# A one-block language-model tower: chunk 2's embedding moved forward, three matmuls without a reader at a seam, and the order of a head's output against the last maximum of its step

## The chip, the cores and the metric

The kernel runs on one core of one Trainium2 chip. The metric is the time of one execution in microseconds (us) as the device measures it. Engines are named as in the profile: PE is TensorE (PEld its weight loads), DVE is VectorE, ACT is ScalarE, POOL is GpSimd, SP is SyncE.

## The reference

The input is 2 samples (b = 0, 1) of 2048 token ids. Shortened to what matters:

```python
h = W.T[x] + bias + positional                       # (2, 2048, 128)
# block 1: 8 heads of 16, causal, linear (no softmax)
qkv  = layernorm(h) @ w_qkv
dots = where(causal, q @ k.T * scale, 0)
attn = (dots - cumulative mean) * rsqrt(cumulative variance + EPS) * norm_g + norm_b
h    = h + (where(causal, attn, 0) @ v) @ w_out + b_out
# block 2: 2 heads of 64, softmax, then 8 soft-gated experts
hx   = layernorm(layernorm(h)) * ln_g + ln_b
q, k = l2norm(hx @ Wq), l2norm(hx @ Wk);  v = hx @ Wv
y    = softmax(causal(q @ k.T * scale)) @ v @ Wo
gate = softmax(y @ gate_W + gate_b)
h    = h + sum_e gate_e * (gelu(y @ W1_e + b1_e) @ W2_e + b2_e)
```

## The kernel before

Each engine has its instruction list written out by hand, and the engines meet at semaphores (`wait_ge` before an instruction, `then_inc` behind it). An engine works its list strictly in order, so an instruction that waits holds up everything behind it in the same list. Tokens are cut into NT = 16 chunks of 128 per sample, and a chunk is always handled for both samples.

**Stage A, first block.** Chunk c goes through `embed` (DVE: position added, `bn_stats`, `bn_aggr`), `front` (POOL: variance to reciprocal root, by a power), `normed` (DVE: the normalised rows `xn`), `xn_T` (PE transposition), projections, masked products, sums over earlier chunks and an output projection. From chunk 1 on `step_a(c)` does one chunk on every engine and prepares the next ones: DVE embeds c+2 inside step c, PE transposes c+1. Chunk 0 is different: its attention is worked out directly, in `dtm`, before the loop begins, and chunk 2 is embedded between chunk 0 and `step_a(1)`. `state_out` (DVE, L656) masks the running sum of keys times values, `state_add` (POOL, L264) adds it up, and `coefs` (POOL, first instruction L268, a power on 128x16) makes the coefficients that `outputs` (DVE, L720 to L727) multiplies with. PE's list at this place holds the last 16 narrow matmuls of chunk 0 for sample 1, `busy(1, 1)`, which multiplies the identity with constants into a bank nobody reads, `xn_T(2, 0)`, and then `step_a(1)`, whose first products don't need chunk 2.

**Seam A to B.** The last chunk of the first block and the first chunks of the second block are interleaved by hand. On PE the order is: 16 narrow matmuls for sample 1 of chunk 15, `project2(1)` (four matmuls of 128x384, waiting until ACT has copied the sums of chunk 15 out of their banks, L435), `out_T(14)`, `normed_T(2)`, `out_project(14)`.

**Stage C, second attention.** The 8 items are (c, b): 512 queries of one sample. They are worked through in NSTEP = 80 steps; step s takes one block of 128 keys for one item (items have 4, 4, 8, 8, 12, 12, 16, 16 steps). The softmax's maxima are worked out ahead of their item by `pair_scores` (PE, both heads, banks 3 and 4) and `row_max` (DVE, L866); MSLOT[s] lists which of them belong to step s. PE's order within step s is: `scores(s)`, the early pairs, `values(s-2)` for both heads (LAG = 2), the closing pairs, `out_part`s; from step CLOSE = 36 on the closing pairs come behind the `out_part`s. How many pairs close a step is worked out by

```python
closing = min(len(pairs), 1) if s >= CLOSE else len(pairs) // 2
```

A pair waits until DVE has taken the maximum of the pair before it, since both use banks 3 and 4. `head_out(it)` (DVE, a reciprocal L941 and a product L943 into `och`) takes an item's output out of banks 6 and 7. It stands at step OAT[it] = 5, 9, 17, 25, 37, 49, 65, 81, the step in which PE does the item's last `values`. The next item's first `values`, one step later, wait for it (`o_used`). On DVE one step is: `out_part(…, 5)` (L933), all `row_max` of the step, `head_out`, `out_part` 3 or 4 (the gate, L915 to L928), then the low halves of the probabilities that are DVE's (L974, L976).

**Stage D.** 64 rounds of experts follow, PE bound; nothing there is touched. L1024 is the helper `mm`, so that nearly all matmuls carry this line.

Of the kernel before, what the change touches and what calls it, by code (L numbers as in the profile page):

```python
# [23 lines left out]
CH = 512  # L24
# [19 lines left out]
def tower(nc, ids, emb_rows, consts, consts16, rows, cols, w_qkv, w_out, w_sm, w_o, w_gate, w12_rows, b2, out):  # L44
    with ExitStack() as ctx:
# [187 lines left out]
        def _(pool):  # L233
# [3 lines left out]
            def gather(t0, t1):  # L237
                for t in range(t0, t1):
                    g.indirect_dma_start(out=h_all[:, t, :], out_offset=None, in_=emb_rows,  # L239
                                         in_offset=bass.IndirectOffsetOnAxis(ap=idx[:, t:t + 1], axis=0)  # L240
                                         ).then_inc(GATHERED[t // B], 16)
# [7 lines left out]
            def front(c, par):  # L249
                pool.wait_ge(S["stats"], c + 1)  # L250
                g.tensor_tensor(rs[par][:], mv[par][:, :, 1], ln_eps, ALU.add).then_inc(S["veps"], 1)
                pool.wait_ge(S["veps"], c + 1)
                g.tensor_tensor(rs[par][:], rs[par][:], mhalf[:, 0:B], ALU.pow).then_inc(S["rstd"], 1)
# [7 lines left out]
            def state_add(c):  # L261
                for b in range(B):
                    pool.wait_ge(S["sgc_ready"], 2 * c + b + 1)
                    g.tensor_tensor(sg[:, b], sg[:, b], sgc[:, b], ALU.add).then_inc(S["sg_ready"], 1)  # L264
# [50 lines left out]
            out_bias(0)  # L315
            out_bias(1)
            gather(6, 16)
            coefs(0)
            state_add(0)
            front(2, 0)  # L320

            def step_a(c, nxt, more=2, tail=True):
                if c >= 3:
# [289 lines left out]
        def _(dve):  # L613
# [93 lines left out]
            link(v.tensor_reduce(sm[:, 1, 1], sq[:, 1], AX, ALU.add))  # L707
            dve.wait_ge(S["sq_act"], 1)
            v.tensor_scalar(sm[:, 3], sm[:, 1], inv0, DOT_EPS, ALU.mult, ALU.add).then_inc(S["var_ready"], 1)
            for b in range(B):  # L710
                state_out(0, b, first=True)

            def outputs(c, cur, first=False):
                dve.wait_ge(S["coef"], c + 1 if c < NT - 1 else NT + 1)
# [68 lines left out]
                    normed(c + 2, cur)  # L783
                h1_out(c - 1)

            embed(2, 0)
            normed(2, 0)
            step_a(1, 0, first=True)
            for c in range(2, NT - 2, 2):
                for u in range(2):  # L790
# [155 lines left out]
            for s in range(NSTEP + LAG + 8):  # L946
                if s == 0:
                    unit_qk(NT - 1)
                    low_qk(NT - 2)
                for m in range(LAST):  # L950
                    if s == YAT[m] + DVE_Y[2]:
                        out_part(m, 5)
                two = MSLOT.get(s, ())
                for part in two if two and two[0][0] not in ALONE else two[:1]:
                    row_max(*part, (0, 1))
                if s == 1:
                    low_qk(NT - 1)
                for it in range(len(ITEMS)):
                    if s == OAT[it]:
                        head_out(it)  # L960
                for m in range(LAST):
                    if s - YAT[m] in DVE_Y[:2]:
                        out_part(m, DVE_Y.index(s - YAT[m]) + 3)
                for i in (2 * s, 2 * s + 1):
                    if s < NSTEP and not on_pool(i):
                        lo = STEPS[s][2] * P
                        if rounded(i):
                            dve.wait_ge(S["s_used"], i + 1)
                        else:
                            dve.wait_ge(S["p_ready"], copies(i))  # L970
                        if i >= PR:
                            dve.wait_ge(S["pv_done"], i - PR + 1)
                        if rounded(i):
                            v.tensor_copy(phi[:, i % PR, lo:], p32[:, i % QR, lo:]).then_inc(S["phi_dve"], 1)  # L974
                            dve.wait_ge(S["phi_dve"], sum(rounded(j) for j in range(i + 1)))
                        v.tensor_tensor(plo[:, i % PR, lo:], p32[:, i % QR, lo:], phi[:, i % PR, lo:], ALU.subtract  # L976
                                        ).then_inc(S["plo_dve"], 1)
                if two and two[0][0] in ALONE:
                    row_max(*two[1], (0, 1))
# [40 lines left out]
        def _(pe):  # L1020
# [71 lines left out]
            def busy(bank, n):  # L1092
                for i in range(n):
                    mm(ps[:, bank, :], ident, cst[:, 0:CH])
# [10 lines left out]
            for b in range(B):  # L1105
# [13 lines left out]
                    at = D + h * XW + DA  # L1119
                    last = mm(ps[:, 5 + b, at:at + DA], dtm[:, b, h], kv[0][:, b, h, DA:2 * DA], start=False)  # L1120
                last.then_inc(S["x_ps"], 1)
            busy(1, 1)
            xn_T(2, 0, first=True)

            def step_a(c, nxt, more=True, first=False):
# [89 lines left out]
            for b in range(B):  # L1215
                pe.wait_ge(S["dt_sb"], 2 * c + b + 1)
                for h in range(HA):
                    at = D + h * XW
                    last = mm(ps[:, 5 + b, at:at + XW], dtm[:, b, h], kv[cur][:, b, h], start=False)
                last.then_inc(S["x_ps"], 1)  # L1220
                if b == 0:
                    project2(0, [1])
            project2(1)
            out_T(NT - 2)
            normed_T(2)
# [188 lines left out]
            for s in range(NSTEP + LAG + 6):  # L1414
                if s < NSTEP:
                    scores(s)
                if s < 2:
                    unit_T(NT - 2 + s)
                for i in range(WARM_C.get(s, 0)):
                    mm(ps[:, 5, :], minus16, c16[:, 0:CH])  # L1420
                lone = [(*part, h) for part in MSLOT.get(s, ()) if part[0] in ALONE for h in range(HS)]
                pairs = [part for part in MSLOT.get(s, ()) if part[0] not in ALONE]
                assert not (lone and pairs)
                closing = min(len(pairs), 1) if s >= CLOSE else len(pairs) // 2
                for part in lone[:1]:
                    lone_scores(*part)
                for part in pairs[:len(pairs) - closing]:
                    pair_scores(*part)
                if s in RAT:
                    max_row(RAT[s])  # L1430
                if LAG <= s < NSTEP + LAG:
                    values(s - LAG, 0)
                for part in lone[1:2]:
                    lone_scores(*part)
                if LAG <= s < NSTEP + LAG:
                    values(s - LAG, 1)
                for f in {NSTEP: (0, 1), NSTEP + 1: (2,)}.get(s, ()):
                    up(0, f)
                for part in lone[2:]:
                    lone_scores(*part)  # L1440
                if s < CLOSE:
                    for part in pairs[len(pairs) - closing:]:
                        pair_scores(*part)
                for m in range(LAST):
                    if s - YAT[m] in PE_Y:
                        out_part(m, PE_Y.index(s - YAT[m]) + 1)
                if s >= CLOSE:
                    for part in pairs[len(pairs) - closing:]:
                        pair_scores(*part)


# [88 lines left out]
    return {0: 1, 1: 7, 2: 5}.get(c, 0)  # L1540


def on_pool(i):
    s = i // 2
    if s >= NSTEP - 18:
        return i % 2 == 0
    return i % 2 == 0 or len(MSLOT.get(s, ())) != 1 or s < 16 or s % 2 == 0
# [86 lines left out]
```

## Time and profile before

| | before |
|---|---|
| median of 3 runs | 835.01 us (833.29 to 840.62) |
| profiled execution | 834.53 us |
| its span, first to last instruction | 832.7 us |
| PE busy | 778.6 us, 94% of the span |
| DVE busy | 703.0 us, 84% |
| ACT, POOL busy | 486.5 us, 337.3 us |
| chain that ended last | PE 75%, DVE 12%, issue 5%, POOL 4%, ACT 3% |
| mean granted PE clock | 0.990 |

The span is the time between the first and the last instruction; the profiled execution's own time holds 1.8 us more, around it. The granted clock is the share of TensorE's full clock that it is allowed, 1.00 for 2.4 GHz and 0.50 for 1.2 GHz. The chain is followed back from the last instruction, at each step to what released it.

### The profile page before, as it was taken

How to read it: one execution, taken by the hardware profiler on the slowest of the kernel's cores; microseconds unless marked ns; L12 is line 12 of the kernel's file. 1: busy time of each engine (PE TensorE's matmuls, PEld its weight loads, DVE VectorE, ACT ScalarE, POOL GpSimd, SP SyncE). 2: the span in 40 equal slices, each digit the busy share in tenths (PEclk: the TensorE clock that was granted, in tenths of full speed). 3: DMA queues.
4: the chain of work that ended last, by engine and by line, in shares of the span. 5: the costliest groups of instructions: out<-in, count | busy, mean ns of one | idle time of the engine just before them, and what ended most of it. 6: DMA issues, size and time to landing. Idle time of an engine off the chain costs nothing.

```text
span 832.7 us, 21068 instructions
## 1 busy us (share of the span) xinstructions
PE 778.6 (94%) x8230; PEld 552.5 (66%) x8230; DVE 703.0 (84%) x1575; ACT 486.5 (58%) x1023; POOL 337.3 (41%) x374
## 2 busy tenths in 40 slices
PE   1999999999988889998899999999999999999997
PEld 1568778877755455555556556777777777777775
DVE  3649988999688776777667999999999999999997
ACT  2435555555388667786878767455555555555553
POOL 6638999877575557665766631000000000000000
PEclk9989999999999999999999999999999999999999
DMA  4200111010000000000000000000000000000000
GB/s 132 55 10 20 39 39 27 26 27 14 1 1 1 26 2 2 3 2 2 2 2 3 2 14 2 13 2 14 2 14 2 5 11 9 7 6 11 2 15 13
DMA packets 9666, 12.09 MB, mean 15 GB/s; under 512 B 1856, under 2 KB 6592, under 8 KB 9568
## 3 DMA queue, kind: packets, MB, share of 16 engines
q1 hardware_dynamic: 8544, 8.65, 3.5%
q0 software_dynamic: 1024, 2.10, 0.9%
q8 instruction: 65, 1.06, 0.5%
q14 instruction: 33, 0.27, 0.1%
HBM read 8.65 MB, written 2.10 MB: 13 GB/s over the span
## 4 chain that ended last, share of the span: by engine, by line
PE 75%; DVE 12%; issue 5%; POOL 4%; ACT 3%; DMA 1%; DVEq 0%; ACTq 0%
PE ps L1024 74%; DVE mx L866 2%; POOL ss L345 2%; DVE room L974 2%; DVE room L976 1%; DVE qkn L820 1%; ACT room L592 1%; POOL sm L268 1%; DVE mx L861 1%; DVE ss L805 1%; DMA h_all<-emb_rows,idx 1%; DVE y L701 1%; DVE och L943 1%; PE ps L1032 0%; PE ps L1052 0%
## 5 line engine op out<-in xcount | busy, mean ns | idle before, releaser
L605 ACT ACTIVATE cst<-ps,col 128x512 f32<-128x512 f32 x256 | 175.6, 687 | 157.8 <-PE ps L1024 157.0
L1024 PEld LDWEIGHTS ps<-arena,sq 128*128 128x128 f16 x3072 | 191.9, 98 | 62.0 <-DVE sq L1005 4.9
L1024 PE MATMUL ps<-arena,sq 128*128 128x128 f16 x3072 | 213.1, 219 | 0.3 <-DVE sq L1005 0.2
L1024 PE MATMUL ps<-y,arena 128*128 128x512 f16 x768 | 207.4, 379 | 0.4 <-issue 0.4
L1005 DVE TENSOR_TENSOR sq<-cst,sq 128x512 f16<-128x512 f32 x256 | 176.3, 689 | 4.5
L384 POOL TENSOR_TENSOR room<-room 128x512 f16<-128x512 f32 (+3 forms) x122 | 123.2, 1029 | 74.8 <-ACT room L592 73.9
L999 DVE CAST sq<-cst 128x512 f16<-128x512 f32 x256 | 109.8, 429 | 7.5 <-ACT cst L605 0.5
L583 ACT ACTIVATE room<-ps 128x512 f32<-128x512 f32 (+3 forms) x160 | 76.7, 533 | 43.3 <-PE ps L1024 42.9
L866 DVE TENSOR_REDUCE mx<-ps 128x2 f32<-128x1024 f32 (+2 forms) x64 | 70.2, 1096 | 36.7 <-PE ps L1024 36.5
L1024 PEld LDWEIGHTS ps<-y,arena 128*128 128x128 f16 x768 | 64.5, 98 | 32.0 <-issue 1.2
L992 DVE SCALAR_TENSOR_TENSOR h_all<-ps,gs,h_all 128x128 f32<-128x128 f32 x256 | 77.2, 343 | 0.4 <-PE ps L1024 0.4
L1024 PEld LDWEIGHTS ps<-v,room 128*128 128x128 f16 x1632 | 55.8, 98 | 31.6 <-issue 13.8
L1024 PE MATMUL ps<-v,room 128*128 128x65 f16 (+1 forms) x1632 | 66.2, 195 | 7.7 <-DVE och L943 5.1
L592 ACT CAST room<-room 128x512 f16<-128x512 f32 (+3 forms) x142 | 72.5, 561 | 0.0
L1024 PEld LDWEIGHTS ps<-room,y 128*128 128x128 f32 x512 | 60.9, 192 | 2.7 <-ACT y L467 1.7
L1024 PE MATMUL ps<-room,y 128*128 128x34 f32 (+1 forms) x512 | 60.0, 272 | 0.5 <-ACT y L467 0.5
L268 POOL TENSOR_TENSOR sm<-sm,mhalf 128x16 f32<-128x16 f32 x15 | 43.6, 2908 | 27.5 <-DVE sm L747 22.1
L1024 PE MATMUL ps<-kh,qh 64*128 64x512 f16 (+3 forms) x160 | 33.2, 354 | 10.4 <-DVE mx L866 8.6
L752 DVE TENSOR_TENSOR y<-ps,cst 128x1024 f32<-128x1024 f32 x30 | 36.3, 1211 | 7.5 <-PE ps L1024 7.5
L976 DVE TENSOR_TENSOR room<-room 128x512 f16<-128x512 f32 (+3 forms) x38 | 36.4, 957 | 3.8 <-ACT room L592 3.1
L1024 PE MATMUL ps<-y,room 64*128 64x512 f32 x128 | 39.1, 694 | 0.0
L239 POOL DMA_INDIRECT h_all<-emb_rows,idx x32 | 31.6, 988 | 10.3 <-issue 7.9
(166 smaller groups left out, 1189.5 us busy)
## 6 DMA issues: line engine op xcount, KB each, us to landing
sq<-w_rows SPq DMA_DIRECT2D x13, 256.0 KB, 2.8
out<-h_all SPq DMA_DIRECT2D x32, 64.0 KB, 1.6
cst<-consts SPq DMA_DIRECT2D x1, 896.0 KB, 5.3
h_all<-emb_rows,idx POOLq DMA_INDIRECT x32, 2.6
hxT<-w_rows SPq DMA_DIRECT2D x2, 256.0 KB, 2.7
cst<-consts SPq DMA_DIRECT2D x1, 398.0 KB, 3.7
c<-consts SPq DMA_DIRECT2D x1, 256.0 KB, 5.2
x<-w_rows SPq DMA_DIRECT2D x1, 256.0 KB, 3.0
```

What stands on the lines that cost most here:

```text
L268: g.tensor_tensor(sm[:, 4], sm[:, 3], mhalf[:].rearrange("p (b h) -> p b h", b=B), ALU.pow).then_inc(S["r_ready"], 1)
L384: g.tensor_tensor(plo[:, i % PR, lo:], p32[:, i % QR, lo:], phi[:, i % PR, lo:], ALU.subtract).then_inc(S["plo_pool"], 1)
L583: a.activation(p32[:, i % QR, lo:], ps[:, i % 3, lo:], ACT.Exp).then_inc(S["s_used"], 1)
L592: a.copy(phi[:, i % PR, lo:], p32[:, i % QR, lo:]).then_inc(S["p_ready"], 1)
L605: a.activation(hid[:, f], ps[:, HBANK[f], :], ACT.Gelu_apprx_tanh, bias=col[:, K_B1 + k:K_B1 + k + 1], scale=1.0 / WS).then_inc(S["hid_rea ...
L752: v.tensor_tensor(dtm[:, b], ps[:, 3:5, :].rearrange("p z (h j) -> p (z h) j", j=P), upper.unsqueeze(1).to_broadcast([P, HA, P]), ALU.mult ...
L866: v.tensor_reduce(mx[:, it % 2, r, kb], ps[:, 3:5, 0:w], AX, ALU.max).then_inc(S["sm_used"], 1)
L976: v.tensor_tensor(plo[:, i % PR, lo:], p32[:, i % QR, lo:], phi[:, i % PR, lo:], ALU.subtract).then_inc(S["plo_dve"], 1)
L992: v.scalar_tensor_tensor(hr, ps[:, EBANK[n % 2], r * D:(r + 1) * D], gs[:, m, r, n % E:n % E + 1], hr, ALU.mult, ALU.add).then_inc(S["eo_u ...
L999: v.tensor_copy(hhi[:, f], hid[:, f]).then_inc(S["hhi_ready"], 1)
L1005: v.tensor_tensor(hlo[:, f], hid[:, f], hhi[:, f], ALU.subtract).then_inc(S["hlo_even" if f % 2 == 0 else "hlo_odd"], 1)
L1024: return t_.matmul(o, l, r, start=start, stop=stop, skip_group_check=True)
```

## The change

Three places are edited.

1. Between chunk 0 and `step_a(1)`: DVE embeds chunk 2 between the two `state_out`s of chunk 0 and normalises it behind the second. POOL does `front(2, 0)`, then `state_add(0)`, then `coefs(0)`; before it was the reverse. PE's `busy(1, 1)` ahead of `xn_T(2, 0)` is gone.
2. At the seam PE gets three matmuls of 128x512 in 16 bit into bank 3, which nobody reads, ahead of `project2(1)`.
3. In stage C DVE does `head_out` before the maxima of the closing pairs of its step, where it did it behind them. PE's list is the same; the closing count has become a function. Only steps that have both a `head_out` and a closing pair come out in another order: steps 9, 17, 37 and 49 (items 1, 2, 4 and 5).

```diff
@@ POOL
             gather(6, 16)
+            front(2, 0)
+            state_add(0)
             coefs(0)
-            state_add(0)
-            front(2, 0)
@@ DVE, end of chunk 0
-            for b in range(B):
-                state_out(0, b, first=True)
+            state_out(0, 0, first=True)
+            embed(2, 0)
+            state_out(0, 1, first=True)
+            normed(2, 0)
@@ DVE, ahead of step_a(1)
-            embed(2, 0)
-            normed(2, 0)
             step_a(1, 0, first=True)
@@ DVE, stage C, step s
-                for part in two if two and two[0][0] not in ALONE else two[:1]:
+                early = 1 if two and two[0][0] in ALONE else len(two) - closing(s)
+                for part in two[:early]:
                     row_max(*part, (0, 1))
...
                 for it in range(len(ITEMS)):
                     if s == OAT[it]:
                         head_out(it)
+                if two and two[0][0] not in ALONE:
+                    for part in two[early:]:
+                        row_max(*part, (0, 1))
@@ PE, end of chunk 0
-            busy(1, 1)
             xn_T(2, 0, first=True)
@@ PE, seam
                 if b == 0:
                     project2(0, [1])
+            for i in range(3):
+                mm(ps[:, 3, :], minus16, c16[:, 0:CH])
             project2(1)
@@ 
+def closing(s):
+    parts = [part for part in MSLOT.get(s, ()) if part[0] not in ALONE]
+    return min(len(parts), 1) if s >= CLOSE else len(parts) // 2
```

## Rows read from the trace of the kernel before

**Rows 1.** Page, part 2: granted PE clock in 40 equal slices, in tenths.
```profile
PEclk9989999999999999999999999999999999999999
```

**Rows 2.** Stretches: start:end, length, PE busy (instructions), granted clock, DMA share, GB/s.
```profile
44.98:51.70 6.72, 6.72 (x18) 0.50 0.00 0
...
60.16:72.07 11.91, 11.91 (x81) 1.00 0.03 7
```

**Rows 3.** Timeline, end of chunk 0 (start, length, engine, line, [idle before <-releaser]).
```profile
38.03 2.94 POOL L268 TENSOR_TENSOR sm<-sm,mhalf 128x16 f32<-128x16 f32 x1 [4.68 <-DVE sm L709]
...
40.75 0.44 DVE L656 TENSOR_TENSOR room<-ps,cst 128x272 f32<-128x272 f32 x1 [2.47 <-PE ps L1024]
...
41.11 0.43 DVE L631 TENSOR_TENSOR h_all<-h_all,cst 128x256 f32<-128x256 f32 x1
...
42.20 0.15 DVE L641 BATCH_NORM_AGGREGATE mv<-st 128x2 f32<-128x6 f32 x1
...
43.00 1.10 PE L1024 MATMUL ps<-cst 128*128 128x512 f32 x2
...
43.58 0.71 POOL L253 TENSOR_TENSOR rs<-rs,mhalf 128x2 f32<-128x2 f32 x1
44.32 0.60 DVE L648 TENSOR_SCALAR room<-h_all,mv,rs 128x128 f32<-128x128 f32 x2 [1.97 <-POOL rs L253]
...
44.98 0.69 PE L1032 MATMUL ps<-cst,room 128*128 128x128 f32 x2 [0.88 <-DVE room L648]
...
54.18 0.42 DVE L720 TENSOR_TENSOR room<-room,sm 128x256 f32<-128x256 f32 x1
```

**Rows 4.** Timeline, seam between stages A and B.
```profile
224.72 0.99 ACT L435 COPY room<-ps 128x400 f32<-128x400 f32 x2
...
225.86 2.90 PE L1024 MATMUL ps<-wsm,hxT 128*128 128x384 f32 x4 [0.67 <-ACT room L435]
...
230.53 1.49 PE L1024 MATMUL ps<-wsm,hxT 128*128 128x384 f32 x4
...
232.51 1.03 PE L1024 MATMUL ps<-c 128*128 128x512 f16 x4
```

**Rows 5.** Timeline around step 37, item 4's head_out.
```profile
383.02 1.22 DVE L866 TENSOR_REDUCE mx<-ps 128x2 f32<-128x1024 f32 x1 [0.49 <-PE ps L1024]
...
384.39 0.69 DVE L943 TENSOR_TENSOR och<-ps,rl 128x512 f32<-128x512 f32 x1
...
385.14 0.91 PE L1024 MATMUL ps<-v,room 128*128 128x65 f16 x24 [1.62 <-DVE och L943]
...
385.42 0.52 DVE L928 SCALAR_TENSOR_TENSOR gs<-gt,gl 128x32 f32<-128x32 f32 x1
...
386.41 1.23 DVE L866 TENSOR_REDUCE mx<-ps 128x2 f32<-128x1024 f32 x1 [0.47 <-PE ps L1024]
```

**Rows 6.** Timeline around step 49, item 5's head_out.
```profile
414.29 1.23 DVE L866 TENSOR_REDUCE mx<-ps 128x2 f32<-128x1024 f32 x1 [1.65 <-PE ps L1024]
...
416.27 0.67 DVE L976 TENSOR_TENSOR room<-room 128x384 f16<-128x384 f32 x1
...
416.41 1.15 PE L1024 MATMUL ps<-v,room 128*128 128x65 f16 x24 [1.62 <-DVE och L943]
416.87 0.68 DVE L933 TENSOR_TENSOR h_all<-ps,h_all 128x512 f32<-128x512 f32 x1
...
418.15 1.23 DVE L866 TENSOR_REDUCE mx<-ps 128x2 f32<-128x1024 f32 x1 [0.60 <-PE ps L1024]
```

**Rows 7.** Stretches behind both head_outs, columns as in the second group.
```profile
416.41:420.53 4.12, 4.12 (x62) 0.59 0.00 0
385.14:387.69 2.55, 2.33 (x57) 1.00 0.02 6
```

**Rows 8.** Timeline around step 10, behind item 1's head_out.
```profile
309.74 0.23 PE L1024 MATMUL ps<-kh,qh 64*128 64x128 f16 x2 [0.78 <-DVE mx L866]
...
310.58 0.91 PE L1024 MATMUL ps<-v,room 128*128 128x65 f16 x24 [0.50 <-DVE och L943]
```

More of the change, by code:

```diff
@@ L1423, in _ @@
                 assert not (lone and pairs)
-                closing = min(len(pairs), 1) if s >= CLOSE else len(pairs) // 2
+                close = closing(s)
                 for part in lone[:1]:
                     lone_scores(*part)
-                for part in pairs[:len(pairs) - closing]:
+                for part in pairs[:len(pairs) - close]:
                     pair_scores(*part)
@@ L1441, in _ @@
                 if s < CLOSE:
-                    for part in pairs[len(pairs) - closing:]:
+                    for part in pairs[len(pairs) - close:]:
                         pair_scores(*part)
@@ L1447, in _ @@
                 if s >= CLOSE:
-                    for part in pairs[len(pairs) - closing:]:
+                    for part in pairs[len(pairs) - close:]:
                         pair_scores(*part)
```

## The prediction

> **What bounds the kernel now.** I read the page first. PE is busy nearly all the time, and the chain that ended last is PE for three quarters, so a gain must take idle time out of PE, or time at the low clock. The clock row shows one slice of 40 at 8 tenths ([rows 1]), 41 to 62 us, which is where edit 1 sits; single slices hide shorter drops, so I asked for the clock by stretches of 1 us over the whole span. Four places are below full clock: from about 44.9 to 51.7, from 225.7 to 229.2, from 416.9 to 420.3, and the last 3 us. The first three begin within about a microsecond of the end of a PE wait or inside one, and each of these waits is at one of the three edits. Then I read the chain in order of time at these places, and the timeline for who queues behind whom.
>
> **Edit 1, end of chunk 0.** In the chain POOL's power of `coefs(0)` (38.03, 2.94 us) is followed by its three small products, `state_add`, and then `front`'s power (43.58, 0.71 us), on which `normed` on DVE waits (1.97 us idle) and on that `xn_T(2)` on PE, at 44.98 after 0.88 us of idleness ([rows 3]). So the reader of chunk 2 waits for work it does not need. New order: `state_out(0, 0)` on DVE is done by about 38.3, `embed(2)` takes 1.24 us (41.11 to the end of the last aggregate at 42.35), so the statistics exist at 39.5; POOL is idle from its last gather until then, and `front` takes about 1.0, to 40.6. `state_out(0, 1)` still waits for PE until 40.75 and ends at 41.19, so the embedding lies in a 2.47 us wait of DVE and costs nothing there. `normed(2)` (0.60) ends at 41.8. PE comes free at 43.00, where the filler now starts, so PE is next to be late, not DVE: `xn_T(2)` starts at 43.0 instead of 44.98, a gain of **1.98**. Removing the filler costs nothing by itself, it lay in the wait.
>
> What is pushed back is `coefs(0)`: behind `front` and both `state_add`s, the second of which waits for `state_out(0, 1)`; it starts at about 42.0 and ends about 3.9 later, at 45.8 (before 41.9). Its reader is `outputs(0)`, which ran at 54.18 and will come at about 49, since two masked products and two `state_out`s stand ahead of it; 3 us of cover. If that cover were gone, PE would wait at `out_T(0)`, which comes about 10 us after `xn_T(2)`. Behind `coefs(0)` on POOL stands `state_add(1)`, whose input exists at about 46.3: covered by 0.5 us.
>
> The clock: after the gap PE works 6.72 us at 1.2 GHz, all of it busy ([rows 2]). From 44.98 to the second step's first product at 60.16 it is 15.18 us. The same list one step later, with one transposition and one step of products, takes 11.91 us at full clock ([rows 2]). Without the gap I take the full clock: **3.27** less. (Check: 6.72 us at half clock is 3.36 us of work.) The bounds of this term are 0, if the clock falls all the same, and 3.27. I take the upper, since later waits of PE at this loop's rate keep the clock. Each step of stage A is PE bound, so both terms last to the seam. Edit 1: 5.25.
>
> **Edit 2, seam.** `project2(1)` waits 0.67 us for ACT's two copies (224.72, 0.99 us) and then its four matmuls need 225.86 to 228.55, 2.69 us until the next one starts. The same four begin at 230.53 and are followed at 231.86, 1.33 us, at full clock ([rows 4]). The three fillers: four of their kind take 1.03 us with the last one's latency, a pitch of 0.22, so three take 0.65, which fills the wait almost exactly. Cost 0, at worst 0.1 if the copies end early. Gain if they keep the clock: 2.69 - 1.33 = **1.36**. All that follows (ACT's squares, DVE's sums, POOL's roots) hangs on this projection and moves with it. Bounds: if the clock falls anyway, the fillers themselves take 3 x 0.43 = 1.3 at half clock against a wait of 0.67, a loss of 0.6.
>
> The trace and the Trainium skill differ here. The row shows a drop beginning 0.55 us into a wait of 0.67 us ([rows 4]). The Trainium skill, page "TensorE: Matmul & The Clock Gate", section "Why this matters for your kernels", allows PE idle gaps several times as long as these before throughput drops. By it neither gap would be a cause, and fillers would buy nothing; the time that this gives is one of the rivals below.
>
> **Edit 3, head_out first.** Two cases. *Steps 9, 17, 37:* the closing pair waits on PE for the early maximum, so DVE is idle 0.49 before the closing maximum (383.02), and `head_out` could fit there; it takes 0.92 (384.16 to 385.08, the product alone 0.69). Put first, it delays the closing maximum by 0.92 - 0.49 + 0.03 = 0.46, and the next item's `values`, now at 385.14 after 1.62 of waiting, can start when the scores before them end, at 383.5, a gain of 1.6 on PE ([rows 5]). But PE meets DVE again at the next pair: DVE ends the closing maximum at 384.63, does the gate's three instructions (end 385.94 now, 0.94 in all) and starts the next maximum at 385.6 instead of 386.41. Of 1.6 us **0.8** is left. At steps 9 and 17 PE has an early pair ahead of `values`: it waits for the closing maximum (309.74) and would wait to 310.2, with `values` right behind it at about 310.45 instead of 310.58 ([rows 8]). **0.1** each; the gain on one side is eaten by the delay on the other. *Step 49:* one pair, behind everything, and DVE idle 1.65 before it (414.29). `head_out` fits in whole, no maximum is delayed, and `values` go from 416.41 to 414.85, 1.56 ([rows 6]). Behind it PE works at a mean clock of 0.59 for 4.12 us, while the same stretch after step 37 took 2.55 at full clock ([rows 7]): another 1.57 if the clock holds. Together 3.1, but DVE is late next: maximum 1.23, low half 0.67, residual 0.68, maximum 1.23 from 414.29 on end at 418.0 ([rows 6]), and only then can PE do the pair that it does at 420.53 now. That leaves **2.5**. Edit 3: 0.1 + 0.1 + 0.8 + 2.5 = 3.5; bounds 0.5 (DVE or ACT take it all back but the least) and 5.
>
> **Sum.** 5.25 + 1.36 + 3.5 = 10.1. Against the profiled execution, 834.53 - 10.1 = 824.4. The median of the runs shown is 0.48 above it, so I forecast **824.9** for the median.
>
> **Rivals.**
> - *Clock drops fall where they fall.* Waits of 1.62 us at 383.5 pass without a drop ([rows 5]), waits of 0.67 don't. If the drops aren't made by these waits, they stay in some form elsewhere; then 3.27 + 1.36 and about 1 of step 49 are lost: 824.9 + 5.6 = 830.5. For it: that comparison, and the page. Against it: three drops, at just these places, and none in 175 us of stage A, where PE has no long wait.
> - *Half of it.* One of the three drops stays, most easily the first, since in front of it PE does 16 matmuls of only 16 columns and the filler is gone; half clock during one more stretch costs 1.4 to 3.3: 826.3 to 828.2.
> - *Stage C gives it back.* Waits for ACT's and POOL's halves of the probabilities take the place of `head_out`'s; edit 3 brings 1: 827.4.
> - *Slower than before.* Without `busy(1, 1)` the narrow matmuls leave PE at 1.2 GHz, and stage A's loop, itself of 16 matmuls of 34 columns at a time, doesn't bring it back. 6.72 us at half clock cost 3.3, so against a gain of 1.98 + 1.36 + 3.5 it decides from 14 us of additional half clock, a little over one step; three steps (36 us) would give 845. Against it: the clock came back within step 1 of this same loop ([rows 2]).
> - *It does nothing at the seam*, because the fillers run at half clock themselves: 824.9 + 1.36 + 0.6 = 826.9.
>
> **How the numbers follow.** About 1% (8.4 us) is what a measurement of this kernel can tell from no change, so faster means below 826.7. The forecast has 0.45, "half of it" and the seam together 0.20, stage C 0.12, drops elsewhere 0.18, slower 0.05. Of the 0.20 half lies below 826.7, of stage C's a third: faster 0.60, same 0.36, slower by over 1% 0.04. The range goes from 822.5 (edit 3 at its upper bound of 5, with a little less than that net) to 831.0, the case of drops elsewhere with half a microsecond of play.
>
> **What the profile after would show.** `xn_T(2)` at about 43.0 without a wait before it, and the first product of step 2 at about 55.0 instead of 60.16, all at clock 1.00. `project2(1)` about 5.2 earlier than 225.86, followed by `out_T` 1.33 later. At step 37 the product into `och` in front of the closing maximum, PE's `values` without a wait, and 0.8 us won by the next maximum; at step 49 the same with about 2.5. Stage D as long as before. Wrong it would be if slices with a clock under 1.00 turn up elsewhere in about the same sum, or if stage C's length stays the same to half a microsecond though the waits on `och` are gone.

## The result, and the profile after

| | before | after |
|---|---|---|
| median of 11 runs each | 837.6 us | 830.3 us |
| ratio, 95% interval | | 0.9902 [0.9875, 0.9928] |
| profiled execution, its span | 834.53, 832.7 us | 829.22, 827.4 us |
| PE busy | 778.6 us | 774.9 us |
| mean granted PE clock | 0.990 | 0.993 |

The ratio is a gain of 8.2 us (6.0 to 10.5); the forecast was a gain of 10.1 (834.53 to 824.4) and a median of 824.9, with a range of 822.5 to 831.0. One disturbed execution of the changed kernel (1553 us) does not count in the ratio; the median of the other ten is 830.2. The median of the kernel before is now 3.1 us above the execution that had been profiled; the runs on chip 2, below, bear on that.

The two profiled executions differ by 5.3 us. Markers that both lists have split this up:

```
                                        before    after   gained up to here
first product of step 2 (PE)             60.16    58.62    1.54
project2(1) begins (PE)                 225.86   225.84    0.02
first product into och, item 0 (DVE)    295.66   294.30    1.36
the same, item 6                        452.84   447.11    5.73
the same, item 7                        486.93   481.62    5.31
```

So in this pair of profiles the seam gave 1.34 (1.36 less 0.02), stage C about 4 (4.37 up to item 6, 3.95 up to item 7), and edit 1 nothing in the end: 1.54 up to step 2, lost again before the seam. The timeline of the changed kernel at the end of chunk 0, which answers to [rows 3] (L1028 and L1036 are L1024 and L1032 of before):

```profile
35.65 0.37 ACT L421 COPY room<-ps 128x256 f32<-128x256 f32 x1 [3.01 <-remote]
...
39.73 1.96 PE L1028 MATMUL ps<-room,y 128*128 128x16 f32 x16 [1.96 <-ACT y L467]
...
40.81 0.72 POOL L253 TENSOR_TENSOR rs<-rs,mhalf 128x2 f32<-128x2 f32 x1
...
41.53 1.69 PE L1114 MATMUL ps<-cst,y 128*128 128x128 f32 x8
...
44.59 0.44 DVE L656 TENSOR_TENSOR room<-ps,cst 128x272 f32<-128x272 f32 x1 [4.14 <-PE ps L1028]
44.95 1.04 DVE L648 TENSOR_SCALAR room<-h_all,mv,rs 128x128 f32<-128x128 f32 x2
...
45.87 2.91 POOL L268 TENSOR_TENSOR sm<-sm,mhalf 128x16 f32<-128x16 f32 x1
...
46.59 0.42 PE L1036 MATMUL ps<-cst,room 128*128 128x128 f32 x2
```

The order is the forecast one: POOL's root at 40.81 long before `normed`, `normed` right behind the second `state_out`, `xn_T(2)` at 46.59 without a wait, and `coefs(0)` from 45.87, last of the three on POOL. But the whole stage is late. ACT idled 3.01 us here, and 1.51 us ahead of the pair of copies before this one, with a releaser that the profile does not know, and PE waited 1.96 us for the copy behind it (in the kernel before it did these sixteen matmuls without a wait). And the clock fell ahead of `xn_T(2)` all the same. Stretches of the changed kernel (start:end, length, PE busy, clock, DMA share, GB/s), against [rows 2] and [rows 4]:

```profile
41.80:45.20 3.40, 3.40 (x16) 0.50 0.04 11
46.59:58.62 12.03, 12.03 (x82) 1.00 0.02 7
...
212.50:215.90 3.40, 3.38 (x16) 0.50 0.00 0
225.84:227.20 1.36, 1.36 (x4) 1.00 0.00 0
458.20:461.60 3.40, 3.40 (x38) 0.51 0.00 0
```

The stretch from `xn_T(2)` to step 2 took 12.03 where 15.18 was spent before. That is the forecast length, but not for the forecast reason: the drop was not avoided, it came at 41.8, ahead of `xn_T(2)`, and slowed the matmuls there. And there are two stretches at 1.2 GHz that the kernel before did not have, at 212.5 and 458.2, and the first costs what had been gained up to step 2. The seam went as forecast, 1.36 us at full clock.

Step 37, which answers to [rows 5], in the changed kernel's timeline of DVE:

```profile
379.52 1.23 DVE L866 TENSOR_REDUCE mx<-ps 128x2 f32<-128x1024 f32 x1 [0.49 <-PE ps L1028]
380.67 0.20 DVE L941 RECIPROCAL rl<-ps 128x8 f32<-128x8 f32 x1
380.90 0.69 DVE L943 TENSOR_TENSOR och<-ps,rl 128x512 f32<-128x512 f32 x1
381.50 1.22 DVE L866 TENSOR_REDUCE mx<-ps 128x2 f32<-128x1024 f32 x1
...
383.06 0.47 DVE L928 SCALAR_TENSOR_TENSOR gs<-gt,gl 128x32 f32<-128x32 f32 x1
383.45 1.21 DVE L866 TENSOR_REDUCE mx<-ps 128x2 f32<-128x1024 f32 x1
```

Step 49, which answers to [rows 6], in the same view:

```profile
410.14 0.69 DVE L943 TENSOR_TENSOR och<-ps,rl 128x512 f32<-128x512 f32 x1
411.31 1.23 DVE L866 TENSOR_REDUCE mx<-ps 128x2 f32<-128x1024 f32 x1 [0.48 <-PE ps L1028]
412.45 0.55 DVE L980 TENSOR_TENSOR room<-room 128x384 f16<-128x384 f32 x1
412.92 0.69 DVE L933 TENSOR_TENSOR h_all<-ps,h_all 128x512 f32<-128x512 f32 x1
413.52 1.22 DVE L866 TENSOR_REDUCE mx<-ps 128x2 f32<-128x1024 f32 x1
```

PE's timeline of the changed kernel at both steps, the next item's first `values`:

```profile
381.68 0.91 PE L1028 MATMUL ps<-v,room 128*128 128x65 f16 x24
382.78 0.39 PE L1028 MATMUL ps<-kh,qh 64*128 64x512 f16 x2 [0.19 <-DVE mx L866]
...
411.75 0.91 PE L1028 MATMUL ps<-v,room 128*128 128x65 f16 x24
```

`values` follow the scores without the 1.62 us of before, at both places, and the next thing that PE waits for is DVE's maximum, as forecast (0.19 us ahead of the pair at 382.78): DVE now has no idle time between `head_out` and the next maximum at step 37.

### The profile page after: what moved, and what is told of

It reads as the page before. It is cut to its first block, busy times and chain, and to the rows that moved or that the text cites. A ratio compares the mean times of both kernels' runs of the same rounds, so it can differ in the third digit from the quotient of the medians.

```text
span 827.4 us, 21070 instructions
## 1 busy us (share of the span) xinstructions
PE 774.9 (94%) x8231; PEld 551.6 (67%) x8231; DVE 700.7 (85%) x1575; ACT 487.1 (59%) x1023; POOL 338.1 (41%) x374
## 4 chain that ended last, share of the span: by engine, by line
PE 76%; DVE 9%; POOL 5%; issue 5%; ACT 4%; DMA 1%; another core or an unknown queue 1%; DVEq 0%; POOLq 0%; ACTq 0%
PE ps L1028 74%; DVE mx L866 3%; POOL room L384 2%; POOL ss L345 2%; DVE qkn L820 1%; ACT room L592 1%; DVE room L980 1%; DVE mx L861 1%; DVE ss L805 1%; DMA h_all<-emb_rows,idx 1%; PE ps L1056 0%; PE ps L1036 0%; ACT room L583 0%; POOL sm L282 0%
## 5 line engine op out<-in xcount | busy, mean ns | idle before, releaser
L1028 PEld LDWEIGHTS ps<-arena,sq 128*128 128x128 f16 x3072 | 191.9, 98 | 62.0 <-DVE sq L1009 4.9
L1028 PE MATMUL ps<-arena,sq 128*128 128x128 f16 x3072 | 213.1, 219 | 0.3 <-DVE sq L1009 0.2
L1028 PE MATMUL ps<-y,arena 128*128 128x512 f16 x768 | 207.4, 379 | 0.4 <-issue 0.4
L583 ACT ACTIVATE room<-ps 128x512 f32<-128x512 f32 (+3 forms) x160 | 76.8, 534 | 39.6 <-PE ps L1028 39.2
L1028 PEld LDWEIGHTS ps<-y,arena 128*128 128x128 f16 x768 | 64.5, 98 | 32.0 <-issue 1.2
L1028 PEld LDWEIGHTS ps<-v,room 128*128 128x128 f16 x1632 | 55.6, 98 | 26.6 <-issue 15.7
L1028 PE MATMUL ps<-v,room 128*128 128x65 f16 (+1 forms) x1632 | 65.7, 195 | 3.0 <-DVE room L980 1.4
L1028 PEld LDWEIGHTS ps<-room,y 128*128 128x128 f32 x512 | 61.3, 193 | 4.4 <-ACT y L467 3.4
L1028 PE MATMUL ps<-room,y 128*128 128x34 f32 (+1 forms) x512 | 60.4, 273 | 2.0 <-ACT y L467 2.0
L1028 PE MATMUL ps<-kh,qh 64*128 64x512 f16 (+3 forms) x160 | 33.0, 352 | 11.6 <-DVE mx L866 9.8
L1028 PE MATMUL ps<-y,room 64*128 64x512 f32 x128 | 36.8, 655 | 0.0
L239 POOL DMA_INDIRECT h_all<-emb_rows,idx x32 | 31.8, 992 | 10.1 <-issue 7.9
```

The costliest lines, as they stand in the source:

```text
L583: a.activation(p32[:, i % QR, lo:], ps[:, i % 3, lo:], ACT.Exp).then_inc(S["s_used"], 1)
L1028: return t_.matmul(o, l, r, start=start, stop=stop, skip_group_check=True)
```

## The experiments

All ratios are against the kernel before on the same chip, with 95% intervals. Each execution lists its span and its mean granted clock; twice the missing share of the clock times the time is how long PE was at 1.2 GHz (rounding leaves 0.8 us of play in one execution, less in a mean). Such time costs about half its length. The means are over 23, 29, 18 and 11 executions of the kernel before, 12 each of e1_start, e2_seam, e5_start_filler, e6_head_late, e7_head_early and e10_before_fill, 7 of e9_fillstart, 6 each of e3_head, e4_all, e11_no_seam and e12_fill_again, and 4 of e8_fill.

```
                                    ratio    95% interval      us, mean   at 1.2 GHz, us, mean
chip 6  before                                                 831.6      14.2
        e1_start   edit 1           0.9972   0.9954-0.9990     829.0      11.8
        e2_seam    edit 2           0.9993   0.9978-1.0009     831.0      12.2
        e3_head    edit 3           0.9947   0.9927-0.9968     827.2       9.9
        e4_all     changed kernel   0.9909   0.9885-0.9934     824.0       8.0
chip 7  before                                                 831.5      14.5
        e5_start_filler             0.9965   0.9951-0.9979     828.5       8.7
        e6_head_late                0.9966   0.9948-0.9983     828.8      15.3
        e7_head_early               0.9984   0.9965-1.0003     829.9      10.4
        e8_fill                     0.9881   0.9854-0.9907     822.1       0.8
chip 2  before                                                 837.6      22.8
        e9_fillstart                0.9924   0.9897-0.9951     831.2      15.2
        e10_before_fill             0.9960   0.9935-0.9984     834.5      15.4
        e11_no_seam                 0.9923   0.9893-0.9953     830.8      13.3
chip 0  before                                                 830.4      12.1
        e12_fill_again              0.9906   0.9882-0.9931     822.8       0.5
```

**Each edit alone, and the whole again.** e1_start, e2_seam and e3_head have the hunks of the diff above for their edit and nothing else; e4_all is the changed kernel.

> Edit 1 alone (chunk 2 embedded sooner, POOL's order, filler gone). Theory 1, as in the prediction: xn_T(2) comes 2.0 us sooner and the low clock behind it goes, 5.25 us in all, ratio 0.9938. Theory 2, after the profile of the changed kernel: the gain is only the earlier start, 1.5 to 2.0 us (ratio 0.9979), because PE falls to 1.2 GHz in this stretch all the same. Theory 3: ACT's two idle stretches before its copies L421 (1.5 and 3.0 us in the changed kernel's profile) are made by the edit; then they show here and the gain is near 0. If they come from the execution and not from the kernel, they are missing here or show in a kernel without the edit.

> Edit 2 alone (three unread matmuls at the seam). Theory 1: project2(1) to out_T 1.33 us at clock 1.00 instead of 2.69 at 0.50, 1.4 us in all, ratio 0.9984. Rival: the low clock is not tied to the 0.67 us wait; then out_T follows project2(1) after 2.7 us as before, or the low clock is missing for other reasons and the fillers bring nothing, 0 us.

> Edit 3 alone (head_out before the closing maximum). Theory 1: 3.5 us (0.1, 0.1, 0.8 and 2.5 at steps 9, 17, 37 and 49), ratio 0.9958; the changed kernel's profile has 3.95 from the first head_out to the last. Rival: half of the gain at step 49 belongs to a clock that fell in one profile only; then 2.0 to 2.5 us, ratio 0.9973.

> The changed kernel again, for a second profile. If ACT's idle stretches at L421 are a matter of the execution, they may be missing; then xn_T(2) starts at about 43.0 and step 2 at about 55.0, as predicted. If they are made by the kernel, they are here again, and step 2 starts at about 58.6. Time 827 to 831 us, ratio 0.990. The sum of the three single edits should be the whole: they touch stages that are 170 us and 60 us apart.

The means fall by 2.6, 0.6 and 4.4 us, together 7.6, and the whole by 7.6: the edits add up, as far as intervals of 1.3 to 2 us each way can tell. Edit 3 is more than half of it; edit 1, which I had put first with 5.25, is 2.6 (0.8 to 3.8). The 0.6 of edit 2 is not told from nothing (its ratio's interval reaches 1.0009), so neither of its theories is decided by the time. ACT's idle stretches are missing in all four, so the edit does not make them (theory 3 is out). e4_all came in under the 827 to 831 us expected, at 824.0, on a chip where the kernel before takes 831.6; in it `xn_T(2)` starts at 40.37 and step 2 at 53.98. e1_start shows edit 1 without them. Its timeline of PE:

```profile
38.20 1.96 PE L1024 MATMUL ps<-room,y 128*128 128x16 f32 x16 [0.47 <-ACT y L467]
40.01 0.60 PE L1032 MATMUL ps<-cst,room 128*128 128x128 f32 x2
40.54 2.08 PE L1024 MATMUL ps<-y,room 64*128 64x512 f32 x4
```

And its stretches, columns as above:

```profile
38.20:40.01 1.81, 1.80 (x16) 1.00 0.38 126
40.01:53.63 13.62, 13.62 (x83) 0.87 0.02 6
205.20:207.52 2.32, 1.87 (x18) 0.97 0.00 0
207.52:210.67 3.15, 3.15 (x14) 0.50 0.00 0
```

`xn_T(2)` follows the sixteen 16-column matmuls at once (1.81 us after their start, where it was 44.98 - 41.19 = 3.79, taking the start of these matmuls, 41.19, from the timeline of before). Yet the clock falls at `xn_T(2)`, with no wait ahead of it but the 0.47 us from before these matmuls. It comes back after one stretch of 3.4 us instead of two, so that step 2 begins 13.62 us later and not 11.91; half of the clock term is there. Then comes a drop at 207.4, in a wait of 0.45 us ahead of `out_T(13)`, and PE needs 167.1 us from step 2 to `project2(1)`. This is so in all three profiles of edit 1 without further fillers (167.14, 167.17, 167.22 us), while the kernel before, e2_seam and e3_head need 165.70 each. That wait is in every one of these versions; the drop was not.

The other profiles show that the first drop is no matter of one execution, nor of the wait behind it. Counted from the start of the last sixteen 16-column matmuls of chunk 0, step 2 begins after

```
old start, drop of 6.83 us   before 18.97   e2_seam 18.75   e3_head 18.59   e6_head_late 18.72
old start, no drop           e7_head_early 16.34
edit 1, drop of 3.41 us      e1_start 15.43   e4_all 15.42
```

So four of these five profiles with the old start have the drop, and edit 1 shortened it but did not remove it: 18.8 became 15.4, a gain of 3.3, of which the new drop at `out_T(13)` took 1.4 to 1.5 back. In e2_seam, e3_head and e6_head_late the clock fell at 41.14, 43.45 and 40.76, that is while PE was in the filler `busy(1, 1)` (from 40.51, 42.76 and 40.02), before the wait ahead of `xn_T(2)` had begun. The filler up to the drop, and from the drop to `xn_T(2)`, in e2_seam:

```profile
40.51:41.14 0.63, 0.63 (x4) 1.00 0.00 0
41.14:43.13 1.99, 0.82 (x2) 0.50 0.00 0
```

**Is it the wait or the filler?** e5_start_filler is e1_start with one line back:

```diff
+            busy(1, 1)
             xn_T(2, 0, first=True)
```

> Edit 1 with the filler busy(1, 1) kept ahead of xn_T(2). Theory A, from the profiles so far: the clock falls because of the 16-column matmuls ahead of this place, with or without a wait, so the filler changes nothing of the clock; it no longer lies in a wait and costs its own length, 0.43 us at full and 0.85 at half clock. Time against edit 1 alone: 0.4 to 0.9 us more, so about 829.6 where edit 1 alone had a mean of 829.0. Theory B: it is the filler that keeps the clock, and its removal took back the gain that I forecast; then PE stays at 1.00 from xn_T(2) to step 2, that stretch is 12.3 us instead of 13.6, and the kernel is 1 us faster than edit 1 alone.

Its profile looks like theory B, its times leave both open. The filler now lies on the path and costs PE 0.94 us, from 41.69 to 42.63 in its timeline, and still the mean is no worse (828.5 against 829.0, on chips whose kernel before has 831.5 and 831.6), with 3 us less at 1.2 GHz. That difference, 11.8 against 8.7, is under twice its standard error (about 1.8, from twelve executions each), and the 1 us of theory B is not reached. In the profile the clock is 1.00 until the last microseconds, and the stretch from `xn_T(2)` to step 2 is 12.0 us:

```profile
42.63:54.63 12.00, 12.00 (x81) 1.00 0.03 7
```

But this execution, with 1.7 us at 1.2 GHz, is the best of the twelve; the others have 6.6 to 16.6. And up to the end of the filler PE does here just what it does in e2_seam, e3_head and e6_head_late, where the clock fell within the filler. So whether the filler keeps the clock at this place is not shown; it may help, and to call its removal free had no ground. What else can happen is in e7_head_early, which has the old start with filler and wait. Its timeline of PE, and then its stretches:

```profile
39.58 1.96 PE L1028 MATMUL ps<-room,y 128*128 128x16 f32 x16 [0.47 <-ACT y L467]
41.38 1.10 PE L1028 MATMUL ps<-cst 128*128 128x512 f32 x2
43.87 0.44 PE L1036 MATMUL ps<-cst,room 128*128 128x128 f32 x2 [1.38 <-DVE room L648]
```

```profile
42.48:43.87 1.39, 0.01 (x2) 1.00 0.00 0
43.87:55.92 12.05, 12.05 (x80) 1.00 0.02 7
```

Here PE waits 1.39 us, longer than in [rows 3], and the clock stays. A wait with no drop, and in e1_start a drop with no such wait: the wait is not what decides by itself. The page "TensorE: Matmul & The Clock Gate" of the Trainium skill, section "Why this matters for your kernels", lets idle gaps of this size pass, and this trace agrees (1.39 us at clock 1.00); but the drop in e1_start, without any such gap, is not in that rule.

**Edit 3, which steps.** e6_head_late and e7_head_early have the new order at steps 37 and 49 only, or at 9 and 17 only:

```diff
-                early = 1 if two and two[0][0] in ALONE else len(two) - closing(s)
+                early = 1 if two and two[0][0] in ALONE else len(two) - (closing(s) if s >= CLOSE else 0)
```

(and `s < CLOSE` for the other).

> Edit 3 at steps 37 and 49 only. By the prediction these two are 3.3 of 3.5 us; by the profile of the changed kernel, too, nearly all, 3.5 of 3.95. Ratio 0.9957 to 0.9960. Rival: half of edit 3's measured 4.4 us comes from steps 9 and 17; then 0.9973.

> Edit 3 at steps 9 and 17 only. Prediction 0.2 us, the changed kernel's profile 0.44 between the first and the fourth head_out: ratio 0.9995 to 1.0. Rival as for the late steps: 2 us, 0.9975.

The means move by 2.8 and 1.6 us, together the 4.4 of e3_head, but the intervals reach from 1.4 to 4.3 and from -0.2 to 2.9, and e7's whole movement is in its time at low clock. The profiles tell it better. The first exponential of each step (ACT, L583), counted from that of step 0, is a clock common to all versions:

```
step                    8      12     18     24     36     40     48     52     64
before              25.22   35.08  53.03  67.30  99.68  110.24 131.37 143.07 170.56
less e3_head         0.00    0.32   0.31   0.44   0.45   1.64   1.64   4.40   4.40
e7_head_early less
e3_head              0.01    0.02   0.01   0.02   0.04   1.23   1.22   2.49   2.50
```

Steps 9, 17, 37 and 49 give 0.32, 0.12, 1.20 and 2.76. In e7_head_early, whose stage C is at full clock without the new order at 37 and 49, step 49 gives 1.27; the other 1.5 is the drop behind step 49 in the kernel before, which one of the six profiles without the new order there has. Edit 3 is 0.32 + 0.12 + 1.20 + 1.27 = 2.9 us of waits. Its timed 4.4 (2.7 to 6.1) includes that and 4.3 us less at 1.2 GHz, about 2.1 us of time.

**Fillers where PE does little.** e8_fill is the changed kernel with two more:

```diff
                 else:
                     pe.wait_ge(S["qkT_sb"], 2)
                     busy(1, 3)
+                if b:
+                    busy(1, 1)
                 pe.wait_ge(S["attnT0_sb"], b + 1)
@@ step_a
+                        if c == NT - 2:
+                            mm(ps[:, 3, :], ident, cst[:, 0:CH])
                         out_T(c - 1)
```

> The changed kernel with two more unread matmuls of 128x512: one in PE's 0.47 us wait ahead of the last 16-column matmuls of chunk 0, one in its 0.45 us wait ahead of out_T(13), where all three profiles of kernels with edit 1 fell to half clock. Theory A (little work in narrow matmuls lowers the clock): the drop at out_T(13) is missing, and the one at xn_T(2) is rarer or later; 1 to 3 us faster than the changed kernel, 821 to 823 us. Rival (drops fall where they fall, or move on): the mean low-clock time stays at 8 us and the time at 823.5 to 824.5.

As theory A has it: 0.8 us at 1.2 GHz on the mean of four executions instead of 8.0, no drop in the profile before the last microsecond, and the lowest time of all, 822.1 us. (That narrow matmuls lower the clock is the theory's reason; the run shows that the fillers help.) The filler ahead of `out_T(13)` is not free: from step 2 to `project2(1)` PE needs 166.0 us, against 165.7 without filler and drop and 167.2 with the drop. Its stretches (from `xn_T(2)` to step 2, around `out_T(13)`, and `project2(1)`) are those of a kernel at full clock:

```profile
42.43:54.46 12.03, 12.03 (x82) 1.00 0.02 7
201.00:215.00 14.00, 14.00 (x89) 1.00 0.00 1
220.46:221.79 1.33, 1.33 (x4) 1.00 0.00 0
```

e9_fillstart has the first of the two only, e10_before_fill is the kernel before with both and the seam's three, e11_no_seam is e8_fill without the seam's three.

> The changed kernel with only the first of the two further fillers, the one ahead of the last 16-column matmuls of chunk 0. If each place is a case of its own, the low clock at xn_T(2) is gone (1.5 us) and the one at out_T(13) stays in a part of the executions; mean low-clock time 3 to 5 us, time about 823. Rival: the two fillers only worked together, and the low-clock time is near 8 us.

> The kernel before with nothing but fillers: the three at the seam, one ahead of the last 16-column matmuls of chunk 0, one ahead of out_T(13). This takes the clock's share out of the comparison. Theory A: the low-clock time falls from 14.5 us to 2 to 5 (stage C's own drops stay), the time by half of that, 5 to 6 us, to 826, ratio 0.993 to 0.994; the difference to the changed kernel with the same fillers (822.1) is then edit 1's earlier start and edit 3, about 2 + 3. Rival: drops move to other places, and the gain is under 2 us.

> The changed kernel with both further fillers but without the three at the seam. If the seam's fillers matter, project2(1) runs at half clock in most executions, 1.4 us each: low-clock time 3 to 4 us and a time of 823.0 to 823.5, against 822.1 with them. Rival: with the other two in place the seam keeps its clock by itself, and the time is 822.1 again.

All three missed what was expected of them (a time of 822.1 to 826 us, and at most 5 us at 1.2 GHz): they met something else, and can't settle what they were made for. On this chip the kernel before takes 837.6 us, as in the first comparison, and in all three profiles ACT idles 4.4 to 4.8 us ahead of its fourth pair of row copies, here in e9_fillstart, in its timeline of ACT and then of PE:

```profile
35.09 0.37 ACT L421 COPY room<-ps 128x256 f32<-128x256 f32 x1 [4.42 <-remote]
```

```profile
33.48 2.31 PE L1028 MATMUL ps<-cst 128*128 128x512 f32 x5
39.16 3.60 PE L1028 MATMUL ps<-room,y 128*128 128x16 f32 x16 [3.38 <-ACT y L467]
42.60 1.95 PE L1114 MATMUL ps<-cst,y 128*128 128x128 f32 x8
```

PE's products for this copy are done by 31.7, so ACT did not wait for them. PE then waits 3.38 us for ACT and does the narrow matmuls at half clock (3.60 us for sixteen, 1.96 at full), before any filler of mine is reached. Ten other profiles (before, e1 to e8, e12) have no such stretch; that of the changed kernel has 1.5 and 3.0 us at the same two copies. With the stall step 2 begins at 60.27 and 59.39 (e9_fillstart, e11_no_seam), without it at 54.46 and 53.93 (e8_fill, e12_fill_again): 4.9 to 6.3 us, the greater part of the 6 to 7 us between this chip and the others. No profile of the kernel before itself shows the stall, so that it slows that kernel here, and is part of the spread in the first comparison, is inferred.

A second thing stands in the way of the plain reading that the fillers end the drops. All three profiles have another stretch of 3.41 us at 1.2 GHz in stage C, from 308.5, 311.6 and 308.8, which costs 1.1 to 1.4 us between steps 8 and 12, and e10_before_fill one more at 465.2. The one of e9_fillstart:

```profile
308.50:311.90 3.40, 3.13 (x50) 0.50 0.00 0
```

e2_seam and e6_head_late have one of 6.83 us at the same place (from 304.0 and 303.6, 1.9 and 2.2 us). None of the fillers of these runs stands near it.

What the three do show: the fillers pay on this chip, too. The kernel before with fillers alone (e10_before_fill) is 3.2 us faster by the means (1.3 to 5.4), with 15.4 instead of 22.8 us at 1.2 GHz, and with edits 1 and 3 (e9_fillstart, e11_no_seam) it is another 3.3 and 3.6 us.

> The changed kernel with both further fillers a second time, since its first measurement has few executions and the chips differ. If the chip is one on which ACT has its unexplained idle stretch of 4 to 5 us ahead of the fourth pair of row copies, PE loses its clock there before any filler runs, and the ratio is 0.992, as with the other two kernels with fillers on such a chip; on a chip without it, 0.988 again with a low-clock time near 1 us.

This is a chip without the stall. The low-clock time is 0.5 us, as expected, the ratio 0.9906, where 0.988 was expected. Together with e8_fill the kernel with both fillers takes 822.1 and 822.8 us, on chips where the kernel before takes 831.5 and 830.4, a gain of 9.4 and 7.6. It beats the kernel before beyond doubt. Against the changed kernel (824.0 where before has 831.6) the means favour it, by its time at low clock, but the intervals of the ratios overlap and the two were never timed on one chip.

## Why the prediction was right, and where not

The direction was right, and the sum was 10.1 for a measured 8.2 (7.6 in e4_all). The time itself was 830.3 where 824.9 was forecast, near the top of the range, and 2.6 of the 5.4 us between them are the kernel before itself, whose median was 835.01 over the three executions known then and 837.6 over eleven. Counted from the 835.01 that the forecast started from, the ratio gives 826.8, which is where "half of it" stands among the rivals, and a hair outside what the prediction had called faster (below 826.7). That the sum came near is in part luck, errors of both signs: timed, edit 1 gave half of its 5.25 and edit 2 half of its 1.36, edit 3 more than its 3.5. By its own steps:

- **Edit 1, the earlier start, 1.98.** Right in its mechanism: POOL, DVE and PE come in the forecast order, nobody waits for the later `coefs(0)` (`outputs(0)` starts at 52.64 in the changed kernel, its last coefficient is done at 49.67), and PE is what comes late next. The size is 3.79 - 1.81 = 1.98 in e1_start.
- **Edit 1, the clock, 3.27.** This is the term that failed: of the 2.6 us that the edit gave, 0.6 is left for it. I took the upper bound because "later waits keep the clock", and the cause was put down to the 0.88 us wait. The clock falls without it (e1_start, e4_all), falls before it has begun (e2_seam, e3_head, e6_head_late) and may stay with it (e7_head_early). What the drop has ahead of it in e1_start is sixteen matmuls of 16 columns, 1.81 us, and a wait of 0.47. With a filler in that wait it was missing in both profiles on chips without the stall (e8_fill, e12_fill_again), and their mean low-clock times say the same of the other executions; with one behind the matmuls it was missing in one profile (e5_start_filler) that is not typical. Of 3.27 about half was left in the profiles without the stall, 15.18 - 13.62 = 1.56, and the new drop at `out_T(13)` took back 1.44 to 1.52 (167.14 to 167.22 less 165.70). So `project2(1)`, forecast 5.2 us earlier, came 0.02 earlier in the changed kernel's profile, behind ACT's late copies and the new drop.
- **Edit 2, 1.36, cost 0.** Right in size where the drop is: 2.69 became 1.36, and the fillers moved `project2(1)` by 0.02 us at most. What I had not asked is how often it is there. Of the profiles without the seam's fillers three (before, e1_start, e7_head_early) have it and four (e3_head, e5_start_filler, e6_head_late, e11_no_seam) don't; of seven with them none has. That is in favour of the fillers, but three against none of seven can be chance. 3/7 of 1.36 is 0.6, and 0.6 was timed, though its interval includes no gain at all. Edit 2's real worth is open between 0 and 1.4.
- **Edit 3, 0.1 + 0.1 + 0.8 + 2.5.** 0.32, 0.12, 1.20 and 2.76 in profiles, together 4.4, with 3.5 forecast and 4.4 timed. Of the 2.76 at step 49, 1.5 is a drop that only the profile of the kernel before has, so that the waits alone are 2.9. That DVE takes over as the bound right behind `head_out` was right. The term for step 37 was too small since I added durations, while in these rows DVE starts an instruction about 0.1 us before the duration of the one before it is over: reciprocal and product took 0.83 to the next start, not 0.92, and the gate 0.81, not 0.94; with the starts of `head_out` and of the gate (0.07 and 0.08 early) that is 0.37 of the 0.4. At step 9 the delayed maximum mattered less than reckoned.
- **Rivals.** "Drops fall where they fall" (0.18) had a real part in it: they moved, to 212.5 and 458.2 in the changed kernel's profile. The prediction's own sign of being wrong, slices under 1.00 elsewhere in about the same sum, came in good part: ahead of the last microseconds the changed kernel's profile has 3 x 3.41 = 10.2 us at 1.2 GHz, the one of before 13.7. It was wrong that they can't be influenced: on two chips five unread matmuls leave 0.8 and 0.5 us of them, while on chip 2 five in the kernel before leave 15.4 of 22.8. "Half of it" (one of three stays) is closest to what happened to edit 1. The filler's removal was named there as what might keep the first drop; e5_start_filler points that way but does not show it. The slower rival did not come: one stretch of 3.4 us, and PE was back at full clock within step 1.

What stays open: why ACT idles at its row copies on some chips (the only transfers in that time are POOL's gathers of embedding rows, which e8_fill has there as well without the idle time, and the releaser is unknown to the profile), why the same list of PE keeps the clock at the first place in one execution and loses it in another, why stage C drops between steps 8 and 12 in five of the fourteen profiles, and why the drop at `out_T(13)` comes in all three profiles with edit 1 as it stands and in none without it. e5_start_filler and e9_fillstart, with edit 1 and one filler more at the start only, don't have it either (165.70 and 165.69 us from step 2 to `project2(1)`), so it seems to depend on something that a filler 165 us earlier shifts; what that is, these runs don't show.

## What to carry to other kernels

A drop of the clock that is seen in one profile beside a wait is not yet caused by that wait, nor is it there in every execution: read the mean clock of all executions first, multiply the price by how often the drop occurs, and look at what PE did ahead of the wait, too. In this kernel fillers inside the waits beside narrow matmuls took most of the low clock away; only all of them together were shown to (e8_fill, e12_fill_again), and one that lies on the path costs its length. Whether an old filler is free to remove should be measured, and not read from the wait that it lies in. And one profile is one execution: compare its clock with that of the others before building on it (e5_start_filler's is the best of twelve). When an instruction that frees a buffer is moved ahead of one that the same engine owes to the next step, trace both readers to the point where they meet again; here 1.6 us won on one became 1.2, and at other steps 0.1 to 0.3.

## What the runs showed of the hardware

- PE kept 2.4 GHz through a wait of 1.39 us (e7_head_early) and fell to 1.2 GHz at `xn_T(2)` with nothing but 0.47 us of waiting and sixteen 16-column matmuls ahead (e1_start). In three profiles it fell while PE was in a matmul of 512 columns behind those sixteen (e2_seam, e3_head, e6_head_late), in two with the same PE list up to there it did not (e5_start_filler, e7_head_early). The low stretches, but for the one in which an execution ends, lasted 3.41, 6.83 or 10.24 us.
- The changed kernel with two fillers more had 0.8 us at 1.2 GHz in a mean execution, where the kernel before has 14.5 (e8_fill), and 0.5 where it has 12.1 on another chip (e12_fill_again).
- Chips differ: 830.4, 831.5, 831.6 and 837.6 us for the kernel before. In every profile taken on the last one ACT stands still for 4.4 to 4.8 us at one place, PE waits 3.4 us and more for it, and its clock is at 1.2 GHz behind that wait.
